# Window attention: transposes in row tiles of 64 tokens, output projection in column tiles, waits gathered ahead of the last score product

## The reference

```python
h = _layernorm(xf, norm1_g, norm1_b)            # 48 channels, windows of 8x8 = 64 tokens
qkv = h @ qkv_w.T + qkv_b                       # 4 heads of 12
attn = einsum('whnd,whmd->whnm', q * scale, k) + bias
attn = softmax(attn, axis=-1)
o = einsum('whnm,whmd->whnd', attn, v)
xf = xf + (o @ proj_w.T + proj_b)               # then layernorm 2, fc1, gelu, fc2, residual
# then: 1x1 convolution to 288 channels, depthwise 3x3, 1x1 back to 48, batch norms, residual
```

## Time and profile before

| | |
|---|---|
| median of 3 runs | 1971.72 us (1970.92 to 1975.22) |
| the profiled execution | 1974.2 us, its span 1972.4 us, granted TensorE clock 0.99 |
| busy over the span | PE 1876.1 us (95%), PEld 1569.7, DVE 1447.1 (73%), ACT 1322.2 (67%), POOL 646.9 (33%) |
| DMA | 198.74 MB, 101 GB/s on the mean |

### The profile page before, as it was taken

How to read it: one execution, slowest core, us unless ns; L and a number is a source line. 1 busy time by engine, 2 the same in 40 slices (tenths; PEclk the granted TensorE clock), 3 DMA queues, 4 the chain that set the end, 5 groups by cost and what they waited for, 6 DMA issues and landing times.

```text
span 1972.4 us, 77068 instructions
## 1 busy us (share of the span) xinstructions
PE 1876.1 (95%) x29960; PEld 1569.7 (80%) x29960; DVE 1447.1 (73%) x2650; ACT 1322.2 (67%) x2838; POOL 646.9 (33%) x869
## 2 busy tenths in 40 slices
PE   5999999999999996999999999989999899999998
PEld 4888888888888885555555898989989898999987
DVE  5999999999999996666667565655656465565554
ACT  2888888888888884555555666656656566666665
POOL 4333333333333334213102352433253343334240
PEclk9999999999999997999999999999999999999999
DMA  2222222222222222777664445544453454454441
GB/s 67 68 77 76 74 76 77 73 76 77 77 73 76 77 75 83 185 180 174 157 152 96 111 104 108 131 104 95 113 120 91 98 135 101 106 132 96 109 99 34
DMA packets 286442, 198.74 MB, mean 101 GB/s; under 512 B 225991, under 2 KB 275672, under 8 KB 276504
## 3 DMA queue, kind: packets, MB, share of 16 engines
q1 hardware_dynamic: 282114, 189.12, 37.9%
q0 software_dynamic: 2368, 6.25, 1.5%
q10 hardware_dynamic: 1750, 0.39, 0.1%
HBM read 128.36 MB, written 54.72 MB: 93 GB/s over the span
## 4 chain that ended last, share of the span: by engine, by line
PE 56%; ACT 2%; issue 1%; DVE 1%; DMA 1%; SPq 0%; ACTq 0%; DVEq 0%
PE psum L1122 14%; PE psum L1141 13%; PE psum L1167 9%; PE psum L680 5%; PE psum L1176 5%; PE psum L661 3%; PE psum L651 3%; PE psum L666 2%; ACT h2T L1223 1%; DVE h L890 1%; DMA room<-tok_mid 0%; DMA room<-in_ident 0%; ACT room L750 0%; DVE room L890 0%; ACT h L889 0%
## 5 line engine op out<-in xcount | busy, mean ns | idle before, releaser
L939 POOL TENSOR_TENSOR mats<-mats,dscale 112x2048 f32<-112x2048 f32 x72 | 260.8, 3622 | 355.6 <-DMA mats<-in_taps 353.5
L1122 PE MATMUL psum<-ew,xp 64*100 64x96 f32 x6144 | 323.3, 253 | 17.8 <-DVE h L890 11.1
L890 DVE TENSOR_SCALAR h<-psum 100x384 f32<-100x384 f32 x384 | 212.0, 557 | 159.8 <-PE psum L1122 148.4
L1223 ACT ACTIVATE h2T<-psum 96x1024 f32<-96x1024 f32 x192 | 195.7, 1020 | 186.4 <-PE psum L1176 186.3
L1122 PEld LDWEIGHTS psum<-ew,xp 64*100 64x100 f32 x6144 | 295.6, 165 | 27.9 <-DVE h L890 14.1
L1141 PE MATMUL psum<-h,mats 101*64 101x128 f32 x4608 | 271.1, 277 | 10.0 <-issue 8.4
L1141 PEld LDWEIGHTS psum<-h,mats 101*64 101x64 f32 x4608 | 254.8, 138 | 19.5 <-issue 10.4
L889 ACT ACTIVATE room<-psum 64x512 f32<-64x512 f32 (+1 forms) x384 | 206.0, 537 | 89.9 <-PE psum L1141 83.3
L344 PE MATMUL psum<-kb,qa 128*64 128x256 f32 x2048 | 244.4, 381 | 0.8 <-DVE prob L443 0.8
L890 DVE TENSOR_SCALAR room<-psum 64x512 f32<-64x512 f32 (+1 forms) x288 | 174.3, 605 | 76.8 <-PE psum L1141 70.8
L889 ACT ACTIVATE h<-psum 100x384 f32<-100x384 f32 x384 | 186.4, 486 | 49.1 <-PE psum L1122 37.0
(11 more groups left out here) (154 smaller groups left out, 3230.4 us busy)
## 6 DMA issues: line engine op xcount, KB each, us to landing
mats<-in_taps SPq DMA_DIRECT2D x69, 896.0 KB, 6.3
tok_mid<-mid SPq DMA_DIRECT2D x128, 224.0 KB, 1.9
room<-tok_mid SPq DMA_DIRECT2D x64, 448.0 KB, 4.4
piece<-img_mid SPq DMA_DIRECT2D x196, 63.8 KB, 2.3
img_mid<-room SPq DMA_DIRECT2D x128, 97.5 KB, 3.1
kb<-kk SPq DMA_DIRECT2D x512, 24.0 KB
out<-yc SPq DMA_DIRECT2D x32, 384.0 KB, 4.4
scratch<-in_x_tokens SPq DMA_DIRECT2D x126, 96.0 KB, 1.9
```

What stands on the lines that cost most here:

```text
L890: return nc.vector.tensor_scalar(dst, src, 0.0, None, ALU.max)
L939: nc.gpsimd.tensor_tensor(m, m, bc(scale[0:MROWS, at:at + TCH], 2, POUT), ALU.mult).then_inc(mats_scaled, 1)
L1122: mm = nc.tensor.matmul(ring[(j + u) % 4][0:PIN, p:4 * CH:4], xp[hx][rows, 2 * j + p, :], w1[rows, c, :], start=True, stop=True)
L1223: nc.scalar.activation(h2T[n % 2][0:CH, :, :], turned_at(n, last)[0:CH, :, 0:POUT * PART], ACT.Copy).then_inc(copied, 1)
```

## The change

- **Transposes in row tiles.** A new helper `turn` replaces each transpose of 128 rows by two of 64 rows (window 0 and window 1 of the pair), which write to two banks. There are 24 of them per step instead of 12, each moving 64 columns instead of 128. The order is now input (i+2), output (i-2), probabilities (i-1), with one `pT_ready` behind all sixteen.
- **Queries and keys behind the transposes**, ahead of the output projection; the projection is cut into column tiles of 64 tokens: four products of 64x98 in place of two of 128x96.
- **Residual's sum from a column.** The projection weights get a 49th column for each half, the sum of the other 48 (`YE = C + 1`, two `tensor_reduce` at the start). So the projection gives each token's sum too. VectorE adds it to the token sum that it has from L420 (`sums` is kept for all groups now), a `tensor_tensor` of 128x4, and the `tensor_reduce` of L457 goes.
- **Waits.** What step i of TensorE needs for its transposes is waited for in one place, `before_turns`, which stands between the seventh and the eighth score product, so ahead of the one that gives `s_ready`.
- **Banks.** `ps_xT` and `ps_oT` take two banks each, `ps_v` moves to the probabilities' first bank, `ps_y` has bank 6 with 4 x 49 columns. ScalarE copies the input's transpose ahead of the output's; `probT` is laid out window by window.

```diff
-        ps_xT, ps_v, ps_y = ps_a[:, 0:TOK // 2], ps_a[:, 0:PAIRS * C], ps_a[:, TOK // 2:TOK // 2 + PAIRS * C]
-        ps_o, ps_oT = ps_b[:, 0:PAIRS * NH * VE], ps_b[:, TOK // 2:TOK]
+        ps_y, ps_v = ps_a[:, 0:PAIRS * YE], psum[:, 2, 0:PAIRS * C]
+        ps_o, ps_oT = ps_b[:, 0:PAIRS * NH * VE], psum[:, 6:8, TOK - P:TOK]
+        ps_xT = psum[:, 4:6, TOK // 2:TOK // 2 + P]
...
+            for e in range(2):
+                nc.vector.tensor_reduce(w_o[:, YE * e + C:YE * e + C + 1], w_o[:, YE * e:YE * e + C], AX_X, ALU.add).then_inc(w_ready, 1)
...
+            def turn(dst, src, col):
+
+                for w in range(2):
+                    rows = slice(NT * w, NT * w + NT)
+                    mm = nc.tensor.transpose(dst[:, w, col:col + NT], src[rows, :, :], ident[rows, rows])
+                return mm
+
+            def before_turns(i, s):
+
+                if has(i + 2):
+                    pe.wait_ge(xn_done, i + 3)
+                    wait(pe, q_copied, i + 2)
+                    wait(pe, k_copied, i + 2)
+                if has(i - 2):
+                    pe.wait_ge(on_done, i - 1)
+                    wait(pe, res_done, i - 2)
+                if has(i - 1):
+                    pe.wait_ge(exp_done, i)
+                    wait(pe, pT_copied, 2 * i - 2)
+                    if has(i):
+                        pe.wait_ge(v_copied, i + 1)
...
                     for n in range(PAIRS * part, PAIRS * part + PAIRS):
                         p, w = divmod(n, 2)
+                        if n == 2 * PAIRS - 1:
+                            before_turns(i, s)
                         mm = nc.tensor.matmul(ps_s[NT * w:NT * w + NT, p // 2, 256 * (p % 2):256 * (p % 2) + 256],
...
+                if has(i + 2):
+                    for a in range(PAIRS // 2):
+                        mm = turn(ps_xT, xn[s][:, 2 * a:2 * a + 2, :], NT * a)
+                    mm.then_inc(xnT_ready, 1)
                 if has(i - 2):
-                    pe.wait_ge(on_done, i - 1)
                     for a in range(PAIRS // 2):
-                        mm = nc.tensor.transpose(ps_oT[:, P * a:P * a + P], on[:, 2 * a:2 * a + 2, :], ident[:, :])
+                        mm = turn(ps_oT, on[:, 2 * a:2 * a + 2, :], NT * a)
                     mm.then_inc(oT_ready, 1)
...
                 if has(i - 1):
-                    pe.wait_ge(exp_done, i)
-                    wait(pe, pT_copied, 2 * i - 2)
-                    turn_probs(i, s, 0)
...
+                    for p in range(PAIRS):
+                        for h in range(2):
+                            mm = turn(ps_p, prob[1 - s][:, NH * p + 2 * h:NH * p + 2 * h + 2, :], NT * (2 * p + h))
+                    mm.then_inc(pT_ready, 1)
...
+                if has(i - 2):
+                    pe.wait_ge(oT_copied, i - 1)
+                    for a in range(PAIRS // 2):
+                        for w in range(2):
+                            mm = nc.tensor.matmul(ps_y[NT * w:NT * w + NT, 2 * YE * a:2 * YE * a + 2 * YE],
+                                                  oT[:, P * a + NT * w:P * a + NT * w + NT], w_o[:, :], start=True, stop=True)
+                    mm.then_inc(y_ready, 1)
...
-                    nc.vector.tensor_tensor(m, ps_y.rearrange("q (p c) -> q p c", c=C), x_of(i - 2), ALU.add)\
-                        .then_inc(res_done, 1)
+                    token_y = ps_y.rearrange("q (p c) -> q p c", c=YE)
+                    nc.vector.tensor_tensor(sums2[s][:, :], token_y[:, :, C], sum_of(i - 2), ALU.add).then_inc(sum2_done, 1)
+                    nc.vector.tensor_tensor(m, token_y[:, :, 0:C], x_of(i - 2), ALU.add).then_inc(res_done, 1)
...
                     dve.wait_ge(res_done, i - 1)
-                    nc.vector.tensor_reduce(sums2[s][:, :], m, AX_X, ALU.add).then_inc(sum2_done, 1)
                     dve.wait_ge(sum2_done, i - 1)
```

More of the change, by code:

```diff
@@ L43 @@
 VE = HD + 1
+YE = C + 1
 MID = 112
@@ L143, in attention @@
         xtok = scratch[:, 0:GROUPS * PAIRS * C].rearrange("q (g p c) -> q g p c", g=GROUPS, p=PAIRS)
-        sums, sums2 = ([sb(f"{n}{s}", [P, PAIRS]) for s in range(2)] for n in ("sum", "sumb"))
+        sums = sb("sum", [P, GROUPS, PAIRS])
+        sums2 = [sb(f"sumb{s}", [P, PAIRS]) for s in range(2)]
         sq_sums, lnv, rstd = (sb(n, [P, 2 * PAIRS]) for n in ("sqs", "lnv", "rstd"))
@@ L197, in x_loads, with sum_of @@
             return 8 * (g - s) + 16
+        def sum_of(g):
+            return sums[:, bass.ds(g, 1), :].rearrange("q g p -> q (g p)")
         def x_of(g):
@@ L347, in scores @@
                         mm.then_inc(s_ready, 1)
+                elif part:
+                    before_turns(i, s)
             def step(i, s):
                 scores(i, s, 1)
+                if has(i + 2):
+                    for a in range(PAIRS // 2):
+                        mm = turn(ps_xT, xn[s][:, 2 * a:2 * a + 2, :], NT * a)
+                    mm.then_inc(xnT_ready, 1)
                 if has(i - 2):
-                    pe.wait_ge(on_done, i - 1)
                     for a in range(PAIRS // 2):
-                        mm = nc.tensor.transpose(ps_oT[:, P * a:P * a + P], on[:, 2 * a:2 * a + 2, :], ident[:, :])
+                        mm = turn(ps_oT, on[:, 2 * a:2 * a + 2, :], NT * a)
                     mm.then_inc(oT_ready, 1)
[L356 to L362, removed]
-                if has(i - 1):
-                    pe.wait_ge(exp_done, i)
-                    wait(pe, pT_copied, 2 * i - 2)
-                    turn_probs(i, s, 0)
[L367 to L373, removed]
-                        mm = nc.tensor.matmul(ps_y[:, 2 * C * a:2 * C * a + 2 * C], oT[:, P * a:P * a + P], w_o[:, :],
-                                              start=True, stop=True)
-                    mm.then_inc(y_ready, 1)
+                if has(i - 1):
+                    for p in range(PAIRS):
+                        for h in range(2):
+                            mm = turn(ps_p, prob[1 - s][:, NH * p + 2 * h:NH * p + 2 * h + 2, :], NT * (2 * p + h))
+                    mm.then_inc(pT_ready, 1)
                 if has(i + 2):
                     pe.wait_ge(xnT_copied, i + 3)
-                    wait(pe, q_copied, i + 2)
-                    wait(pe, k_copied, i + 2)
                     for a in range(PAIRS // 2):
@@ L386, in step @@
                     mm.then_inc(qk_ready, 1)
-                elif has(i):
-                    pe.wait_ge(v_copied, i + 1)
+                if has(i - 2):
[5 more added lines that the diff above has]
+                    mm.then_inc(y_ready, 1)
                 if has(i - 1):
@@ L399, in step @@
                 if has(i + 1):
-                    wait(pe, res_done, i - 1)
                     for a in range(PAIRS // 2):
@@ L419, in step @@
                     dve.wait_ge(x_loaded[s], x_loads(i + 4, s))
-                    nc.vector.tensor_reduce(sums[s][:, :], x_of(i + 4), AX_X, ALU.add).then_inc(sum_done, 1)
+                    nc.vector.tensor_reduce(sum_of(i + 4), x_of(i + 4), AX_X, ALU.add).then_inc(sum_done, 1)
                 if has(i - 2):
@@ L438, in step @@
                     dve.wait_ge(sum_done, i + 5)
-                    nc.vector.scalar_tensor_tensor(cen[s][:, :, :], bc(sums[s][:, :], 2, C), -1.0 / C, x_of(i + 4),
+                    nc.vector.scalar_tensor_tensor(cen[s][:, :, :], bc(sum_of(i + 4), 2, C), -1.0 / C, x_of(i + 4),
                                                    ALU.mult, ALU.add).then_inc(cen_done, 1)
@@ L481, in step @@
                     last.then_inc(v_copied, 1)
+                if has(i + 2):
+                    act.wait_ge(xnT_ready, i + 3)
+                    nc.scalar.activation(by_window(xnT[s][:, :]), ps_xT.rearrange("q w (a t) -> q w a t", t=NT), ACT.Copy)\
+                        .then_inc(xnT_copied, 1)
                 if has(i - 2):
                     act.wait_ge(oT_ready, i - 1)
-                    nc.scalar.activation(oT[:, :], ps_oT, ACT.Copy).then_inc(oT_copied, 1)
-                if has(i + 2):
-                    act.wait_ge(xnT_ready, i + 3)
-                    nc.scalar.activation(xnT[s][:, :], ps_xT, ACT.Copy).then_inc(xnT_copied, 1)
+                    nc.scalar.activation(by_window(oT[:, :]), ps_oT.rearrange("q w (a t) -> q w a t", t=NT), ACT.Copy)\
+                        .then_inc(oT_copied, 1)
                 if has(i + 3) or has(i - 3):
```

25 lines of the change are left out of this document (10 added, 15 removed).

## The result

The changed kernel takes 2000.38 us (median of 4 runs, 1998.39 to 2003.14) beside 1972.51 us (1970.92 to 1975.22) for the kernel before on the same chip: ratio 1.0134 [1.0114, 1.0154], slower. Forecast were +58 us; it is +28. The sign, the place and the mechanism came as forecast, the size did not. The profiled execution took 2003.1 us, 2001.3 of them span.

What follows compares the result with a forecast made beforehand. TensorE was taken to set the 5.65 us step, VectorE just behind; 5.65 + 0.68 (round trip) - 0.22 (sum) = 6.11 us, +0.46 us over 126 steps, 58 us: 2030 us against 1971.7, range 2000 to 2058.

Steps and rivals of the forecast that it cites:

- Direction and mechanism: Slower (chance 0.87), by a TensorE-VectorE round trip ahead of the eighth score product; step between 5.85 and 6.35 us (0.80).
- The round trip's parts: From L423 to the maximum: 0.34 + 0.05 + 0.47 (four waits) + 0.63 (eighth product) + 0.05 = 1.54 us, against 0.86.
- VectorE's sum: On VectorE, L457's 0.39 us goes and a 128x4 sum of 0.17 us comes: 0.22 us a step saved.
- cheap waits: Lower end of the range: waits near the documentation page's figures, +0.22 us a step, 2000 us.
- The second circle: Eighth product waits for v_copied: maximum, exp, ScalarE's value copies, product; 5.5 to 5.6 us, a floor that doesn't decide.
- the first circle: Round trip from `on` on VectorE over TensorE's eighth score product to the maximum, setting the step at 6.11 us.
- stays hidden: Rival: the four waits cost nothing and the sum is small; step 5.54 us, 1958 us, chance 0.06.
- no difference: Rival: the four waits cost nothing, the sum takes 0.17 us or more; step 5.64 us, 1971 us, chance 0.06.
- Transposes: On TensorE, twelve pairs in row tiles take 0.77 us in place of 1.37; 0.60 us a step goes.
- Projection: On TensorE, four column-tiled products like the values' 0.36 us, against 0.51; 0.15 us a step goes.
- Tiling change: On TensorE, one of three changes of tiling per step goes, about 0.10 us.
- The clock: Rival: TensorE's idle time halves its clock to 1.2 GHz, attention some 500 us longer, chance 0.01.

Runs made afterwards that it cites:

- e3_before_waits_ahead: The kernel before with only its waits for on_done, xn_done, v_copied, exp_done and pT_copied put ahead of the eighth score product: 2053.56 us, step 6.28 us.
- e4_reduce_again: The changed kernel with the residual's sum again by tensor_reduce over 128x192, behind the queries' copy, in place of the 128x4 sum: 2057.64 us, step 6.33 us.
- e9_four_more_waits: The changed kernel with four more waits, for counters full since the start, ahead of the eighth score product: 2026.78 us, step 6.07 us.
- e2_on_behind: The changed kernel with only the on_done and res_done waits moved to just ahead of the output's transposes, with a one-column carrying product: 1996.77 us, step 5.80 us.
- e11_values_first: The changed kernel with all before_turns waits behind the eighth score product and the next group's values products ahead of probabilities times values: 1951.12 us, ratio 0.9882.
- e5_reduce_early: The changed kernel with tensor_reduce over 128x192 for the residual's sum, placed with a wait ahead of the queries' copy: 2041.37 us, step 6.20 us.

## Why the prediction was partly wrong

- *Direction and mechanism: right.* The waits ahead of the eighth product put a round trip into the step. e3_before_waits_ahead shows it alone, +0.63 us a step; forecast was +0.68. e4_reduce_again, the whole change but for the sum, stands at 6.33, +0.68.
- *The round trip's parts: right.* 1.52 us on average (1.55 and 1.49) against 1.54; from `on`'s end to the load 0.53 (0.47 in the loop's other step) against 0.52, product and start of the maximum 0.68 against 0.68. The fulfilled waits cost 0.10 each by e9_four_more_waits, taken as 0.12. The Trainium skill's Advanced Engine Details and Errata, section Network/Comms, gives 50 to 100 ns for reading a semaphore: the measured price lies at its upper end.
- *The step that failed: "VectorE's sum", 0.22 us saved.* It measured 0.43 to 0.45. First, the 128x4 sum takes a slot of 0.07 us, not 0.17: I went by the nearest size, but the reciprocal is another operation. That is 0.10 us. Secondly, with the reduction goes the exposed branch in every second step, 0.22 us there, 0.11 to 0.13 on average. I had read one of the loop's two steps fully and of the other only `on` and the maximum. With both, 0.66 - 0.32 - 0.11 = +0.23, which is the 0.225 measured.
- *Luck.* The 2000.4 us lie just inside the range, whose lower end stood for cheap waits. The waits were not cheap; the sum was worth twice what I took.
- *The second circle, "a floor of 5.5 to 5.6": too low,* and nearly the one that decides. e2_on_behind has it at 5.80, since ScalarE's queue lies on it; without the 0.08 us that I put down to its carrying product it would be 5.7, an estimate. It had no effect on the number only because the first circle came out at 5.87. With a cheap round trip this floor would still have held the step above the 5.65 of before, so the rivals "stays hidden" (5.54) and "no difference" (5.64) had no room.
- *Transposes: right.* 0.81 us against 0.77. *Projection: right*; in e11_values_first, where nothing waits, it takes 0.39 us start to start (404.97 to 405.36) against 0.36. *Tiling change:* the loads still pause 0.39 us ahead of the first transpose, part of it the wait for the last score product; what one change less gave wasn't measured apart. That all of it turns into idle TensorE came as forecast.
- *The clock: right.* It stayed at 1.00 though TensorE stands still 37 of 615 us, 0.35 in each step. The Trainium skill's TensorE: Matmul & The Clock Gate, section Part 1: The HAM clock gate, warns of long idle gaps between matmuls. The trace doesn't speak against that: gaps of 0.35 us left the clock at 1.00.

## What to carry to other kernels

Ahead of a product that another engine waits for, put only the waits that this product needs: each of them, fulfilled or not, is on the path (0.10 us), and one that hangs on that other engine makes a round trip of every step. When a change frees the bounding engine, look for the next wait in its own order of work: here the waits behind the product turned +1.3% into +0.7%, and one independent product moved into the next wait turned that into -1.2%. Read every step of an unrolled loop, and give an instruction that needs its neighbour's result some distance ahead of a branch.

## What the runs showed of the hardware

- TensorE's sequencer takes fulfilled waits one by one, at 0.10 us on the mean for an instruction whose record shows 51 ns; four waits for constants made two instructions (e9_four_more_waits).
- A VectorE instruction that waits for the one right ahead of it, with the loop's branch behind it, makes the next three 0.22 to 0.25 us later in all (before, e4_reduce_again); with one copy of 0.68 us between, nothing is lost (e5_reduce_early). That it is the branch is read from its place in the sequencer's rows.
- A VectorE sum of 128x4 elements holds the next instruction back by only 0.07 us, though its record shows 0.15 (after).
